# Mask term and maximum of the attention scores in one VectorE instruction per head

## What is computed

```
def attention(q, k, v, mask):
    scores = einsum('bhqd,bhkd->bhqk', q, k) / sqrt(HD)
    scores = scores * mask - 10000.0 * (1.0 - mask)
    probs = softmax(scores, axis=-1)
    return einsum('bhqk,bhkd->bhqd', probs, v)

# decoder layer, per batch of 16
x = x + self_attention(layernorm(x)) @ w_ao + b_ao
x = x + cross_attention(layernorm(x), encoder) @ w_co + b_co
x = x + gelu(layernorm(x) @ w1 + b1) @ w2 + b2
# RWKV layer on the result: token shift, five mixed streams, decay, key, value, receptance, gate,
# a state recurrence over the tokens, group norm, output projection, then its feed-forward part
```

## Time and profile before

| | |
|---|---|
| median of 3 executions | 694.92 us |
| lowest, highest | 691.0, 696.01 us |
| span of the profiled execution | 694.0 us |
| TensorE matmul busy | 645.3 us (93%) |
| VectorE busy | 598.2 us (86%) |
| ScalarE busy | 571.7 us (82%) |
| GpSimd busy | 311.6 us (45%) |
| mean granted TensorE clock | 0.985 |

### The profile page before, as it was taken

One profiled execution on the slowest core, in us unless ns is written; L12 is line 12 of the kernel. 1 busy time (PEld: TensorE's weight loads), 2 busy tenths in 40 slices (PEclk: granted clock), 3 DMA queues, 4 the chain that ended last, 5 costly groups with the idle time before them and its releaser, 6 DMA issues.

```text
span 694.0 us, 17297 instructions
## 1 busy us (share of the span) xinstructions
PE 645.3 (93%) x5877; PEld 561.6 (81%) x5877; DVE 598.2 (86%) x1430; ACT 571.7 (82%) x2071; POOL 311.6 (45%) x440
## 2 busy tenths in 40 slices
...
GB/s 306 325 70 9 2 104 36 70 70 58 88 9 138 1 146 1 145 2 122 25 85 62 67 81 53 93 4 144 1 146 1 146 0 108 31 70 0 69 9 8
DMA packets 53725, 50.44 MB, mean 73 GB/s; under 512 B 6030, under 2 KB 48902, under 8 KB 53254
## 3 DMA queue, kind: packets, MB, share of 16 engines
...
...
## 4 chain that ended last, share of the span: by engine, by line
PE 80%; DVE 8%; ACT 7%; issue 3%; POOL 1%; DMA 0%; SPq 0%; DVEq 0%; ACTq 0%; POOLq 0%
PE PS_B L552 16%; PE PS_T L654 9%; PE PS_B L694 8%; PE PS_S L552 7%; PE PS_D L559 5%; PE PS_S L625 4%; PE PS_T L662 4%; PE PS_S L559 4%; PE PS_T L559 4%; ACT SC L1291 3%; PE PS_D L800 2%; PE PS_B L703 2%; PE PS_D L552 2%; ACT PT L1301 2%; PE PS_T L545 2%
## 5 line engine op out<-in xcount | busy, mean ns | idle before, releaser
L1291 ACT ACTIVATE SC<-SC,NMX 128x128 f32<-128x128 f32 x512 | 200.0, 398 | 0.2
L1291 ACT ACTIVATION_READ_ACCUMULATOR SC<-SC,NMX 128x1 f32 x512 | 101.0, 197 | 0.0
L654 PE MATMUL PS_T<-CST,SC 128*128 128x128 f32 x512 | 81.3, 281 | 7.7 <-ACT PT L1301 3.6
L976 DVE TENSOR_REDUCE NMX<-SC 128x4 f32<-128x512 f32 x128 | 85.2, 676 | 0.4 <-POOL SC L1499 0.3
L1301 ACT ACTIVATE PT<-PS_T 128x512 f32<-128x512 f32 x120 | 70.8, 590 | 12.7 <-PE PS_T L654 12.7
L654 PEld LDWEIGHTS PS_T<-CST,SC 128*128 128x128 f32 x512 | 56.4, 141 | 26.1 <-ACT PT L1301 12.7
L1057 DVE TENSOR_TENSOR_SCAN SS<-W,AJ 128x1024 f32<-128x1024 f32 x32 | 73.2, 2288 | 0.2
L552 PE MATMUL PS_B<-MX,W 128*128 128x128 f32 x512 | 64.2, 280 | 4.7 <-ACT KR L1350 4.7
L552 PEld LDWEIGHTS PS_B<-MX,W 128*128 128x128 f32 x512 | 61.3, 196 | 4.9 <-ACT KR L1350 4.9
L1499 POOL TENSOR_TENSOR SC<-SC,MADD 128x512 f32<-128x512 f32 x48 | 59.9, 1276 | 6.5 <-DVE SC L956 6.5
L552 PE MATMUL PS_B<-B_LT,W 128*128 128x128 f32 x512 | 61.1, 278 | 1.0 <-ACT B_LT L1231 0.9
...
## 6 DMA issues: line engine op xcount, KB each, us to landing
...
```

The costliest lines, as they stand in the source:

```text
L654: last = pe.transpose(PS_T[:, j * T:(j + 1) * T], SC[:, nr(b, a) % 2, g, j, :], ident)
L976: dve.tensor_reduce(NMX[:, nr(b, a) % 2, GH * g:GH * g + GH], SC[:, nr(b, a) % 2, g], AX_X, ALU.max, negate=True)\
L1291: last = act.activation(SC[:, nr(b, a) % 2, g, j, :], SC[:, nr(b, a) % 2, g, j, :], ACT.Exp, bias=NMX[:, nr(b, a) % 2, h:h + 1], accum_out ...
```

## The change

All groups now go one way. a_mask always leaves its product in PSUM, in place. a_addmask is gone from VectorE and from GpSimd. a_maxima issues four instructions per group, one for each head: each forms -(score + term) from PSUM and MADD into SC, and the minimum of that along the keys (which is the negated maximum) into NMX. a_exps takes the exponential with scale -1. TensorE's scores_read now waits for a_maxima of the group (a_max), for all groups. The wait on the transposes of the attention before last (a_turned), which guards SC, moves from a_mask to a_maxima. The term of the self mask is built by GpSimd at the start.

```
 def scores_read(pe, n, g):
     if n >= 0:
-        b, a = turn_of(n)
-        if (a, g) in DVE_ADDS:
-            pe.wait_ge(a_dadded, nth(DVE_ADDS, b, (a, g)))
-        else:
-            pe.wait_ge(a_masked, 4 * n + g + 1)
+        pe.wait_ge(a_max, 4 * n + g + 1)
...
 def a_mask(b, arg):
...
-    masked = PS_S[:, g] if arg in DVE_ADDS else SC[:, nr(b, a) % 2, g]
-    dve.tensor_tensor(masked, PS_S[:, g], over_heads(mask), ALU.mult).then_inc(a_masked, 1)
+    dve.tensor_tensor(PS_S[:, g], PS_S[:, g], over_heads(mask), ALU.mult).then_inc(a_masked, 1)
...
 def a_maxima(b, arg):
     a, g = arg
-    if arg in DVE_ADDS:
-        dve.wait_ge(a_dadded, nth(DVE_ADDS, b, arg))
-    else:
-        dve.wait_ge(a_added, nth(POOL_ADDS, b, arg))
-    dve.tensor_reduce(NMX[:, nr(b, a) % 2, GH * g:GH * g + GH], SC[:, nr(b, a) % 2, g], AX_X, ALU.max, negate=True)\
-        .then_inc(a_max, 1)
+    dve.wait_ge(a_masked, 4 * nr(b, a) + g + 1)
+    if not later(b, a):
+        dve.wait_ge(set_self, 2)
+    if a:
+        dve.wait_ge(a_less, b + 1)
+    if nr(b, a) > 1:
+        dve.wait_ge(a_turned, 4 * nr(b, a) + g - 7)
+    less = MADD[:, b % 2 if a else 2, :]
+    for j in range(GH):
+        h = GH * g + j
+        last = dve.tensor_tensor_reduce(SC[:, nr(b, a) % 2, g, j, :], PS_S[:, g, j, :], less, -1.0, FAR,
+                                        ALU.add, ALU.min, NMX[:, nr(b, a) % 2, h:h + 1])
+    last.then_inc(a_max, 1)
...
 def a_exps(b, arg):
...
-        last = act.activation(SC[...], SC[...], ACT.Exp, bias=NMX[...], accum_out=SUM[...])
+        last = act.activation(SC[...], SC[...], ACT.Exp, scale=-1.0, bias=NMX[...], accum_out=SUM[...])
```

```
+DVE_ORDER = [
...
+    ("a_mask", (0, 1), 1.005882), ("a_maxima", (0, 0), 1.088235), ("a_mask", (0, 2), 1.135294),
+    ("a_mask", (0, 3), 1.182353), ("a_maxima", (0, 1), 1.217647), ("a_maxima", (0, 2), 1.370588),
+    ("a_maxima", (0, 3), 1.488235),
...
+    ("a_sum", 1, 3.452941), ("b_stats", 0, 3.464706), ("b_moments", 0, 3.476471), ("a_query", 1, 2.500000),
...
+    ("d_output", 0, 5.100000), ("d_means", 0, 5.111765), ("d_centre", 0, 5.123529), ("d_spread", 0, 5.158824),
...
+def in_order(order, moved):
+    turns = [(b + moved.get((name, arg), {}).get(b, turn), name, arg, b) for name, arg, turn in order for b in range(B)]
+    return [(name, arg, b) for _, name, arg, b in sorted(turns, key=lambda t: t[0])]
```

More of the change, by code:

```diff
@@ L87 @@
 SP_ORDER = [
-    ("b_vspread", 0, 4), ("d_store", 0, 6), ("b_wspread", 0, 3), ("b_vstore", 0, 3), ("a_load", 0, 0)]
-PE_ORDER = [
[L90 to L99, removed]
@@ L100 @@
-DVE_ORDER = [
[L101 to L118, removed]
@@ L119 @@
-ACT_ORDER = [
[L120 to L132, removed]
@@ L133 @@
-POOL_ORDER = [
[L134 to L140, removed]
+    ("a_load", 0, 0.900000), ("b_wspread", 0, 3.500000), ("b_vstore", 0, 3.700000), ("b_vspread", 0, 4.100000),
@@ L409, in tiles, with run @@
             return ap.rearrange("p (t n) -> p t n", t=CT)
[L411 to L415, removed]
+        def run(pieces, order, moved):
+            for name, arg, b in in_order(order, moved):
+                pieces[name](b, arg)
         def nr(b, a):
@@ L519, in _ @@
             pieces = named(a_load, b_vstore, b_vspread, b_wspread, d_store)
-            for i in range(B + LAG):
-                run(pieces, SP_ORDER, i)
+            run(pieces, SP_ORDER, SP_MOVED)
             sp.wait_ge(stored, 16 * B)
@@ L864, in _ @@
                            d_own, d_read, d_oturn, d_yturn, d_biasout, d_out, d_turn, d_keyrec, d_val)
-            for i in range(B + LAG):
-                run(pieces, PE_ORDER, i)
+            run(pieces, PE_ORDER, PE_MOVED)
         @block.vector
@@ L949, in a_mask @@
                     dve.wait_ge(in_rows, IN_ROWS)
-                if nr(b, a) > 1 and arg not in DVE_ADDS:
-                    dve.wait_ge(a_turned, 4 * nr(b, a) + g - 7)
                 if not later(b) and a and g == 0:
@@ L1210, in d_mixing @@
                 dve.scalar_tensor_tensor(RR[:, :], RR[:, :], 1.0, dbank(b)[:, 0:C], ALU.add, ALU.mult).then_inc(d_f, 1)
-            pieces = named(a_stats, a_moments, a_normal, b_normal, d_normal, a_key, a_query, a_mask, a_addmask, a_maxima, a_prob_copy, a_inverse, a_context, a_sum,
+            pieces = named(a_stats, a_moments, a_normal, b_normal, d_normal, a_key, a_query, a_mask, a_maxima, a_prob_copy, a_inverse, a_context, a_sum,
                            b_stats, b_moments, b_sum,
```

130 lines of the change are left out of this document (88 added, 42 removed).

## The result

The changed kernel takes 903.99 us (median of 4 runs, 902.94 to 905.3) against 693.69 us: 1.302 times as long, interval 1.298 to 1.306. Forecast were 887 us, in a range of 815 to 935. The profiled execution has a span of 902.0 us, 208.0 more than before, at a mean granted clock of 0.913.

What follows compares the result with a forecast made beforehand. TensorE was taken as the bound, its stops counting whole. Stops in full frames 137, ramp-up 18, clock 40, GpSimd's addition -3: 192 us on a 694.0 us span, giving 887 us with the span-to-median difference; range 815 to 935.

Steps and rivals of the forecast that it cites:

- The bound, and the mechanism: TensorE never waits in the steady state, so its new waits for score banks go whole into the time.
- The new instruction, 0.30 us: VectorE's 128x128 instruction with second result: 0.20 plus 0.10 us start to start, 1.2 us per group of four.
- A: TensorE's a_enc_turn waits for a_maxima (0, 1), which stands behind d_output on VectorE: 5.6 us a frame.
- B: TensorE's a_query of the cross attention waits for a_maxima (0, 3), behind a_sum, b_stats and b_moments: 2.4 us.
- C: TensorE's a_turn of the self attention waits for a_maxima (1, 0): 2.9 us a frame.
- D: TensorE's a_query of the self attention waits for a_maxima (1, 3): 0.85 us a frame.
- a_key's hidden 0.4: Cross attention's a_key needs a_maxima (0, 2); about 0.4 us, covered by the 5.6 us stop at a_enc_turn.
- The clock: Low granted clock after TensorE's stops: 1.7 us for a_enc_turn, 0.85 each for cross a_query and a_turn; 40 us total.
- Rival 1: The clock stays up despite the stops: 847 us, or 823 with the cheap instruction; chance 0.12.
- half of 11.75 each: Three ramp-up frames lack the d_ pieces, so each gets half a frame's stops: 18 us (0 to 35).
- Rival 3: Only VectorE's load counts, banks come back in time: 1.8 us in some 16 frames, 724 us; chance 0.09.
- Rival 4: Faster: new instruction at 0.20 us, TensorE's frame stays 37.24, GpSimd's 1.3 us leave ramp-up and end: 689 us; chance 0.03.

Runs made afterwards that it cites:

- 1: Changed kernel with the mask product written to SBUF, the new instruction working there, and score banks given back at the product: 724.02 us, ratio 1.042.
- 2: Changed kernel with the same places, order and waits, but a_maxima done by two 128x512 instructions, addition then reduction, instead of the four new ones: 959.88 us, ratio 1.382.
- 7: Changed kernel with five a_maxima pieces moved earlier in VectorE's table, so that all banks should come back in time: 735.46 us, ratio 1.058.
- 3: Changed kernel with one piece moved in VectorE's table, a_maxima (0, 1) to right before d_output: 828.75 us, ratio 1.194.
- 4: Changed kernel with each group's four new instructions issued twice, the second four behind a wait on the first: 1031.32 us, ratio 1.485.
- kernel 5: Changed kernel with 18 extra unused TensorE matmuls while a_enc_turn would wait for its bank, batches 3 to 14: 875.02 us, ratio 1.262.
- 9: Kernel with the mask product in SBUF, with two of three Newton steps of the head norm's inverse root left out: 722.00 us, ratio 1.039.
- 12: Kernel with the mask product in SBUF, with the cross attention's a_query put ahead of a_maxima (0, 3) on VectorE: 714.32 us, ratio 1.028.

## Why the prediction came out right

**The bound, and the mechanism.** Right. Any stop of TensorE goes into the time whole; undoing the wait alone (1) gives back 180 of 210 us, keeping the waits without the instruction (2) loses 266 us, and the order alone (7) gives back 169. Three of the signs named beforehand are there: the frame (51.17 us), VectorE's share (28.60 of 40, 0.72) and the low stretch after a_enc_turn.

**The new instruction, 0.30 us.** Mis-sized: 0.21 from start to start. I added 0.10 for the second result from ScalarE's row. That row was misread too: worked like VectorE's rows, with one Gelu record at 0.383 us, a plain one comes every (1.14 - 0.38) / 3 = 0.25 us, so the second result costs ScalarE 0.14. On VectorE the read is a record of its own, as the rule on accumulator outputs in "VectorE: DVE Perf Modes" of the Trainium skill (section on two Vector instructions) says, but it costs nothing: the plain neighbour's 0.20 was the price. A group is 0.85 instead of 1.2 us.

**The stops.** A 5.6 forecast and 5.14 measured, B 2.4 and 2.23, C 2.9 and 2.65, D 0.85 and 0.51; in sum 11.75 and 10.5. The places and the gaps read off the old trace were right. The smaller group alone, five times 0.35 us, would have taken off 1.75; only 1.2 are missing, because the rest of A and of B was put some 0.2 us too short. a_key's hidden 0.4 "without cover" showed in kernels 3, 4 and 7, as 0.19, 0.83 and 0.38 us.

**The clock.** 3.4 us in a full frame forecast, 3.6 read off. The split was wrong: 1.7 for A (measured 1.9), 0.85 for B (1.7) and 0.85 for C (nothing). That the low clock is the default no row here shows: in the first 10 us of the kernel before the granted clock is 1.00, with TensorE busy for 4.8 us. Rival 1, the clock stays up, is what kernel 5 makes in six of eleven frames: 29 us below the changed kernel.

**The sum.** Two errors cancel for the most part, and that is luck: 19.5 us too many in the twelve frames, 33.5 too few in ramp-up. For the twelve frames I had 137 us of stops and 40 of clock, 177, measured 157.5: 1.2 us less in each of eleven, 13, and 4.3 us instead of 10.6 in the twelfth. The twelfth has no stop A, which I had counted: TensorE reaches a_enc_turn at 785.34 without a wait, since the last cross attention follows that of the batch before, with no self attention between them. For ramp-up I had 18 us, "half of 11.75 each" and no clock, measured 51.5. Part of that is a matter of counting: it has the frame before the first that I counted, which is a full one (129.56 to 181.40, 51.8 us, against 37.6 from 92.29 to 129.87 in the kernel before, so 14.3 more). The other 37.2 are stops of 28.3 - 2.6 = 25.7 and the 11.3 us of the low clock. Ramp-up has few batches in flight, but the chain scores, product, maxima, next attention is whole there, so halving it was wrong. The 3 us that GpSimd's addition should give back show at most in the 1 us less behind the last frame.

**Rivals.** Rival 3, only VectorE's load, had 724 us. Kernel 1 gives just that figure, but not by its reason: with the banks back in time the loss comes from small waits (9, 12), not from load. That coincidence is a warning against taking a number for a mechanism. Rival 4, faster, had the cheap instruction right, 0.21 us, and its condition, banks back in time, is the one of kernels 1, 7 and 12; even then the kernel is 3 to 6% slower than before.

**What stays open.** What makes the last 20 us of kernel 12 (7.6 up to its first full frame, 12 in the twelve frames, of which eleven take 1.26 us more each, 0.9 after them), and whether a full retuning of VectorE's table with the new instruction would reach 694. Of the versions tried none beats the kernel before.
